# Second attention: keys copied once by ScalarE and spread over the heads by GpSimd; masks handed over by their banks

## What is computed

```python
    def _L2_xattn_ref(query, key, value, Wq, bq, Wk, bk, Wv, bv, Wo, bo):   # 16 heads of 8
        q = (query @ Wq.T + bq).reshape(B, T, H, D).transpose(0, 2, 1, 3)
        k = (key @ Wk.T + bk).reshape(B, S, H, D).transpose(0, 2, 1, 3)
        v = (value @ Wv.T + bv).reshape(B, S, H, D).transpose(0, 2, 1, 3)
        scores = jnp.einsum('bhtd,bhsd->bhts', q, k) / np.sqrt(D)
        scores = scores + causal[None, None]
        attn = jax.nn.softmax(scores, axis=-1)
        out = jnp.einsum('bhts,bhsd->bhtd', attn, v)
        return out.transpose(0, 2, 1, 3).reshape(B, T, E) @ Wo.T + bo
```

## Time and profile before

| | before |
|---|---|
| median of 3 runs | 862.83 us (862.62 to 863.03) |
| profiled execution | 861.2 us, span 859.1 us |
| TensorE busy | 809.4 us (94%) |
| VectorE busy | 625.2 us (73%) |
| ScalarE busy | 581.3 us (68%) |
| GpSimd busy | 271.1 us (32%) |

### The profile page before, as it was taken

One profiled execution on the slowest core, in us unless ns is written; L12 is line 12 of the kernel. 1 busy time (PEld: TensorE's weight loads), 2 busy tenths in 40 slices (PEclk: granted clock), 3 DMA queues, 4 the chain that ended last, 5 costly groups with the idle time before them and its releaser, 6 DMA issues.

```text
span 859.1 us, 20341 instructions
## 1 busy us (share of the span) xinstructions
PE 809.4 (94%) x7364; PEld 563.9 (66%) x7364; DVE 625.2 (73%) x1588; ACT 581.3 (68%) x1645; POOL 271.1 (32%) x571
## 2 busy tenths in 40 slices
PE   9999999999999999899999999999888889899986
PEld 8887888888888986544444444444555564676652
DVE  5677777777777565676785786685877667799876
ACT  3666676776777766776545585545788879778664
POOL 4355445544444444210000000002034230344455
PEclk9999999999999999999999999999999999999999
DMA  8700000000000000000000000000000000000000
GB/s 339 160 2 2 1 2 2 2 2 1 1 2 2 2 1 2 1 1 0 1 1 0 1 2 0 1 1 0 23 7 3 4 2 1 2 4 3 3 19 34
DMA packets 7887, 13.54 MB, mean 16 GB/s; under 512 B 4342, under 2 KB 5100, under 8 KB 7532
## 3 DMA queue, kind: packets, MB, share of 16 engines
q1 hardware_dynamic: 7788, 12.24, 4.5%
HBM read 11.19 MB, written 1.05 MB: 14 GB/s over the span
## 4 chain that ended last, share of the span: by engine, by line
PE 60%; DVE 13%; ACT 12%; POOL 8%; issue 5%; DMA 0%; DVEq 0%; POOLq 0%; SPq 0%; ACTq 0%
PE psum L1564 10%; PE psum L772 6%; PE psum L812 4%; POOL rstd L520 3%; PE psum L755 3%; PE psum L2018 3%; PE psum L764 3%; ACT arena L2096 3%; POOL arena L1100 2%; PE psum L1573 2%; DVE negmax L1010 2%; PE psum L1550 2%; PE psum L840 2%; ACT arena L910 2%; PE psum L2526 2%
## 5 line engine op out<-in xcount | busy, mean ns | idle before, releaser
L517 POOL TENSOR_TENSOR ve<-mv,epsv 128x1 f32<-128x1 f32 x176 | 36.4, 207 | 508.4 <-DVE mv L512 508.4
L1564 PE MATMUL psum<-arena,w1f 128*128 128x512 f32 x240 | 109.5, 592 | 0.0
L520 POOL TENSOR_TENSOR rstd<-ve,epsv 128x1 f32<-128x1 f32 x176 | 101.7, 578 | 13.8
L910 ACT ACTIVATE arena<-psum,negmax 128x128 f32<-128x128 f32 x256 | 90.5, 408 | 22.2 <-DVE negmax L1010 22.2
L1564 PEld LDWEIGHTS psum<-arena,w1f 128*128 128x128 f32 x240 | 45.5, 190 | 48.7 <-issue 44.3
L1100 POOL TENSOR_TENSOR arena<-arena,rsum 128x512 f32<-128x512 f32 x64 | 65.3, 1040 | 5.6 <-DVE rsum L1016 5.6
L910 ACT ACTIVATION_READ_ACCUMULATOR arena<-psum,negmax 128x1 f32 x256 | 63.4, 248 | 0.0
L1010 DVE TENSOR_REDUCE negmax<-psum 128x8 f32<-128x1024 f32 x32 | 39.2, 1225 | 32.9 <-PE psum L812 32.7
L755 PE MATMUL psum<-arena,sclA 128*128 128x128 f32 x512 | 62.5, 275 | 0.1
L772 PE MATMUL psum<-arena 128*128 128x512 f32 x128 | 61.3, 598 | 0.7 <-DVE arena L1005 0.4
L840 PE MATMUL psum<-prjB,arena 128*128 128x128 f32 x512 | 59.9, 275 | 0.0
(11 more groups left out here) (376 smaller groups left out, 1968.4 us busy)
## 6 DMA issues: line engine op xcount, KB each, us to landing
w<-in_w0qk SPq DMA_DIRECT2D x2, 512.0 KB, 5.0
w<-in_w0vo SPq DMA_DIRECT2D x1, 1024.0 KB, 7.6
cT<-in_cT SPq DMA_DIRECT2D x1, 1024.0 KB, 15.8
out<-x_tok SPq DMA_DIRECT2D x4, 256.0 KB, 2.2
rows<-in_rows SPq DMA_DIRECT2D x1, 836.0 KB, 12.3
x_tok<-in_x_tok SPq DMA_DIRECT2D x1, 768.0 KB, 9.8
ctx_tok<-in_ctx_tok SPq DMA_DIRECT2D x1, 768.0 KB, 10.8
wa<-in_wa SPq DMA_DIRECT2D x1, 768.0 KB, 17.4
```

The source lines that it names most:

```text
L520: pool.tensor_tensor(rstd[:, u, self.i:self.i + 1], ve[:, u, self.i:self.i + 1], epsv[:, 1:2], ALU.pow) \
L910: m = nc.scalar.activation(e0[:, b, g, :], ps(k, P, j * P), ACT.Exp, bias=negmax0[:, b, g:g + 1], accum_out=sum0[:, b, g:g + 1])
L1564: nc.tensor.matmul(ps(k), w1("e2", j * 384 + arg * D, j * 384 + (arg + 1) * D), f1_Hm[:, n, 2 * j + i, :], start=False, stop=False)
```

## The change

1. ScalarE's "qk" of the second attention writes the keys once, with the plain bias, to a new pair of tiles `kT2` (128x128 each). `bk2` and its VectorE instruction go.
2. GpSimd gets a new kind "km": one product of 128x512 that spreads `kT2` over four copies and multiplies by `head4`. It waits until ScalarE has released the bank of keys and queries, and until the scores of two tiles before are done. Its semaphore `a2_spread` is a new wait of TensorE before the scores. Its place is lag 2 in `ATT_POOL`, behind "root" and ahead of "tail", and in `POOL_END` three stand before the root of tile 5 and one behind its bias.
3. ScalarE no longer waits for its own mask copies and raises no `f1_kept`; VectorE waits for the bank of the mask in its place.

```diff
-        POOL_END = [..., ("root", 4), ("own", 4), ("root", 5), ("own", 5)]
+        POOL_END = [..., ("root", 4), ("own", 4), ("km", 0), ("km", 1),
+                    ("km", 2), ("root", 5), ("own", 5), ("km", 3)]
-        ATT_POOL = [("root", 0), ("tail", 7), ("bias", 8), ("own", 1)]
+        ATT_POOL = [("root", 0), ("km", 2), ("tail", 7), ("bias", 8), ("own", 1)]
...
                 nc.scalar.activation(f1_mask[n][MASKS.index(arg)], ps(k), ACT.Copy).then_inc(free[k], 1)
-                stored(act, f1, f"m{it}{arg}", t)
-                act.sem_inc(f1_kept, 1)
...
                 if it == 0:
-                    dve.wait_ge(f1_kept, held(c, arg))
+                    stored(dve, f1, f"m{it}{arg}", t)
...
                     stored(pe, a, "qk", t)
                     if n == 3:
                         kept(pe, "K", t)
+                    else:
+                        pe.wait_ge(spread, t.times(1, 1))
...
                     if n == 2:
-                        if t.n == 0:
-                            act.wait_ge(a_half, 4)
-                        for h in range(QUAD):
-                            nc.scalar.activation(km[:, u, :, h, :], ps(k, P, P).rearrange("p (b k) -> p b k", b=2), ACT.Identity,
-                                                 bias=bk2[:, h:h + 1], scale=head4[:, h:h + 1])
+                        nc.scalar.activation(kT2[:, u, :], ps(k, P, P), ACT.Identity, bias=vec("a2_bk"))
                     nc.scalar.activation(qT2[:, u, :], ps(k, P), ACT.Identity, bias=bqs[:, n - 1:n], scale=DH2 ** -0.5).then_inc(free[k], 1)
...
+                if kind == "km":
+                    u = t.n % 2
+                    stored(pool, a, "qk", t)
+                    if t.n == 0:
+                        pool.wait_ge(a_half, 2 * (n - 1))
+                    if t.n >= 2:
+                        filled(pool, a, "s3", t - 2)
+                    pool.tensor_tensor(km[:, u, :, :, :], kT2[:, u, :].rearrange("p (b k) -> p b k", b=2).unsqueeze(2).to_broadcast((P, 2, QUAD, S)),
+                                       head4.unsqueeze(1).unsqueeze(3).to_broadcast((P, 2, QUAD, S)), ALU.mult).then_inc(spread, 1)
```

More of the change, by code:

```diff
@@ L1294, in build @@
                    ("max", 1), ("s", 1), ("own", 5), of_prev("Z"), of_last("G"), ("apply", 5), of_last("Z")]
-        POOL_END = [("root", 0), ("root", 1), ("own", 0), ("own", 1), ("root", 2), ("root", 3), ("own", 2), ("own", 3), ("root", 4), ("own", 4), ("root", 5), ("own", 5)]
+        POOL_END = [("root", 0), ("root", 1), ("own", 0), ("own", 1), ("root", 2), ("root", 3), ("own", 2), ("own", 3), ("root", 4), ("own", 4), ("km", 0), ("km", 1),
+                    ("km", 2), ("root", 5), ("own", 5), ("km", 3)]
         END_BANKS = {("ha1A", PREV): 7, ("ha1B", PREV): 5, ("f21", PREV): 4, ("hh1", LAST): 5, ("f110", LAST): 6, ("f111", LAST): 7,
@@ L1491, in build @@
         F1_CLOCK = {('L', 0, 0, None): 4, ('H', 2, 0, 's'): 7, ('H', 3, 0, 's'): 3, ('F', 3, 1, None): 5, ('Z', 3, 1, None): 4}
-        f1_masked, f1_kept = sem("f1_masked"), sem("f1_kept")
+        f1_masked = sem("f1_masked")
         spare = [arena[:, 16384:16896], mat(rows, ROWS, "f0_s1"), mat(rows, ROWS, "f0_s2"), ctx_tok[:, 1792:2048],
@@ L1501, in masked @@
             return len(MASKS) * [at for at, *_ in turns()].index((c, it)) + MASKS.index(arg) + 1
-        def held(c, arg):
-            return len(MASKS) * c + MASKS.index(arg) + 1
         def f1_pe(pe, x):
@@ L1904, in build @@
         bk3 = sb("bk3", [P, QUAD])
-        bk2 = sb("bk2", [P, QUAD])
         v3_built = sem("v3_built")
@@ L1963, in attention @@
             max2 = carve(2 * H2).rearrange("p (u h) -> p u h", u=2)
+            kT2 = carve(2 * P).rearrange("p (u k) -> p u k", u=2) if late else None
             assert used["n"] <= (24 * C1 if late else ARENA - (2 * 2 * HALF * 18 + HALF + QUAD)), used
             maxed, exped, inverted, spent = (sem(f"a{n}_{x}") for x in ("max", "exp", "rsum", "spent"))
+            spread = sem("a2_spread") if late else None
             def on_pe(pe, kind, n_tile):
@@ L2177, in dve_build @@
                 nc.vector.tensor_scalar(bk3[:, :], head4, vec("a3_bk"), None, ALU.mult).then_inc(a_half, 1)
-                nc.vector.tensor_scalar(bk2[:, :], head4, vec("a2_bk"), None, ALU.mult).then_inc(a_half, 1)
                 nc.vector.tensor_copy(Vx.rearrange("p u g (r c) -> p (u g) r c", c=9)[:, :, :, DH2],
```

## The result

| | before | after |
|---|---|---|
| median of runs, side by side | 862.73 us (862.43 to 863.03, 4 runs) | 849.61 us (849.10 to 850.99, 4 runs) |
| profiled execution | 861.2 us, span 859.1 us | 850.01 us, span 848.0 us |

The ratio is 0.985, with a 95% interval of 0.9833 to 0.9868. In a second comparison it was 0.9854 (0.9827 to 0.9881; 849.31 us in 6 runs). The forecast was 851.0 us, with a range of 848.8 to 855.3. Single executions of one kernel differ by up to some 5 us, in part because the granted clock of TensorE falls for some 3 us in some of them (experiment 6), so small effects are read from places in the traces.

The account below looks back on a forecast made before the run. Waits between engines bound the second attention: 2.80 us on TensorE plus 2.93 on ScalarE per round of 5.73. Gains of 9.9 (steady part), 1.6 (beginning) and 0.3 (masks) make 11.8: 862.8 - 11.8 = 851.0 us, range 848.8 to 855.3.

Parts of the forecast that it names:

- rival without contention: Second attention: the product slides behind "apply", rounds of 4.79 us and 2.1 gained at the beginning: 849.6 us; chance 0.15.
- costliest case inside the range: Product of 1.5 us on GpSimd and a starved first product at the beginning, both: 854.7 us; rival's chance 0.22.
- ScalarE's loop: Second attention: four key copies become one, 1.38 to about 0.26 us, so the loop falls from 5.73 to 4.61 us.
- TensorE's and VectorE's loop: Second attention: transposes, residual sum, masks, scores, values and back to transposes; the next loop to set the round, 4.79 us.
- round with "apply" held: Second attention: VectorE's L526 held until GpSimd's product is done, 0.74 us later, making VectorE's round 4.99 us.
- mean of the nine rounds from t4: Second attention: rounds of 4.79 and 4.99 us alternate, mean 4.89 us, for nine rounds.
- first three rounds together: Second attention's first three rounds, with no outgoing tile yet: estimated at 4.7 us each.
- t1 to t13: Second attention, tile 1's transposes to tile 13's: 12 rounds from 68.02 to 58.1 us, 9.9 gained.
- product on GpSimd: Second attention: the new 128x512 product with both inputs broadcast takes 1.04 us, 1.5 at the range's upper side.
- beginning, to t1: Start of the second attention: 0.55 us gained at L1587 and 1.1 from tile 2's keys, gain 1.6.
- masks: ScalarE's mask copies unguarded: gain 0.3 us at the first chunk, none in three chunks, bounds 0 and 0.7.
- The rival in which GpSimd is the bound: Second attention: mean round 3.30 + (K+1.4)/2, over 5.73 us from product time K = 3.4; about 866 us at K = 4.1; chance 0.04.

Follow-up runs that it names:

- experiment 6: Changed kernel with three small moves (product a tile later, second product late, clock-keeping products 5 to 2): 849.02, again 848.95 us; changed kernel rerun, giving its second trace: 849.31 us.
- experiment 7: No new kernel: TensorE's pause in the last round (5.52 us instead of 4.92), read from the traces of before, the changed kernel and the other runs.
- Experiment 2: Changed kernel with further ScalarE activations of the old keys' form per tile, written where nobody reads: one 850.43 us, three 863.72 us.
- experiment 3: Changed kernel with the keys' product at lag 3 in ATT_POOL instead of 2, for the tile after next: 850.74 us, ratio 0.9852 to before.
- Experiment 4: Changed kernel with each GpSimd keys' product made several times into the same place: twice 853.67 us, three times 873.47 us, four times 892.12 us.
- second product late: Changed kernel where, at the beginning, GpSimd makes the second tile's product only after VectorE's first row maximum: 849.95 us.

## Why the prediction was right

Its total, 11.8 us, stands beside 12.2 us of span in the second trace (859.1 to 846.9); the forecast for the profiled execution, 849.4, beside 849.03 there. The first trace gained 11.1 us of span, and would have gained some 12.7 without its fall of the clock (1.7 us, experiment 6). The medians moved by more, 13.1 us: the sum took over that the median lies 1.6 us above an undisturbed execution, as it does before, and the changed kernel's medians lie 0.6 and 0.3 above it (849.61 and 849.31 against 849.03). Why the changed kernel's runs lie closer to it is open.

The time alone does not confirm the mechanism. The measured 849.61 is the very number of the rival without contention (849.6), which the traces refute: VectorE's L526 is held in each round up to 665 us. The two forecasts differ by 1.4 us, less than single executions do, so it is the rows below that decide. The upper end of the range, 855.3, is not worked out in the prediction; its costliest case inside the range gives 854.7. By its own terms, the measured column from the first trace of the changed kernel:

| term | forecast | measured |
|---|---|---|
| ScalarE's loop | 4.61 | 4.60, from 4.95 less 0.35 and 5.65 less 1.05 of added work |
| TensorE's and VectorE's loop | 4.79 | 4.69 to 4.72 |
| round with "apply" held | 4.99 | 4.92 |
| mean of the nine rounds from t4 | 4.89 | 4.78 |
| first three rounds together | 14.1 | 14.09 (4.46 4.57 5.06) |
| t1 to t13 | 9.9 gained | 10.9 gained |
| product on GpSimd | 1.04 | 1.04; 1.12 and 1.14 beside VectorE's products |
| beginning, to t1 | 1.6 gained | 1.28 gained (1.96 less the 0.68 that was there) |
| masks | 0.3 gained | 0.47 gained |
| last round | 0 | 0.6 lost |

That the first three rounds add up to 14.1 is luck: none of them is the 4.7 of the estimate. The last round was put at no change; what lengthened it is the pause of experiment 7.

**The steady part.** The mechanism held at each step: ScalarE's four copies left the loop, the second loop took over, "apply" was held for the product and the rounds alternated. Experiment 2 shows the first step in numbers: the loop that no longer binds was sized to 0.02 us. The term that was mis-sized is the second loop. Of its stretches L576 and the masks came where the sum had them (t+1.50 and t+2.97 in the round from 661.72), but L2008 at t+4.55 and not at t+4.62, the 0.07 us by which 4.72 falls short of 4.79; the row that was shown as a check, +4.73 at 688.70, was nearer to the truth, and I kept the sum instead of the row. In the held round L576 comes at t+1.70, and all the rest is 0.2 later. Over nine rounds these 0.07 to 0.09 us are 0.7 of the 1.0 us by which the gain was put too small. The rest is that in this trace the alternation ends at 662 us, where VectorE has no incoming tile's statistics left; I had let it run through all nine.

The Trainium skill, "SBUF — State Buffer", section "SBUF: two separate sides", says that GpSimd and VectorE share one pair of ports as an exclusive lock, held for the whole instruction by whichever starts first, and wanted by VectorE only in a two-port mode or with two SBUF inputs. The trace agrees in the main: L526 0.34 to 1.06 us, L1789 and L1790 0.69 to 1.41, none ending before the product, while L2120, which reads PSUM and SBUF, stays at 1.23. It does not show which of the two conditions L526 meets; that one has a single data input in SBUF. And it does not show that the one that starts first goes first: with lag 3, L526 began 0.07 us ahead of the product and was held, while the product took its 1.04 us (experiment 3); in the earlier trace rows, 0.17 us ahead, it was not.

**The beginning.** The three steps to L1584 were right: first scores at 603.74, which is 604.42 in the times of before (604.35 forecast; 0.68 are the shift that was there), VectorE's chain 1.44 us longer (1.35 forecast), 0.49 gained at L1584 (0.55 forecast), and the two products did slip in between VectorE's. What was missing is the pause of 0.43 us in front of L1596; no row of before showed it. With it TensorE's shift is back at -0.67 there, so that all of the 0.49 was given back. The keys of the third tile then gave 1.3 us, a little more than the 1.1 forecast, and that is nearly all of the 1.28: that the total came near 1.6 is in part luck.

**The masks.** 0.47 instead of 0.3, inside the bounds; one step at the first chunk and none in the others, as argued. The spacing of the copies was put at 0.54 us and is 0.48.

**The rival in which GpSimd is the bound** was priced wrongly, though it did not come to pass. Its formula let the product's time into every second round only. Experiment 4 shows it in every round, K + 2.98. The point from which the round is longer than before is K = 2.75 us by that, not 3.4, and K = 1.5, the upper bound that I took for the product, would have cost nothing in this way (4.48, still below 4.70). The chance I gave it, 0.04, rested on the 3% spread of the product in the earlier trace rows, and that was the right row: 14 of the 16 products took 1.04 us.

## What to carry to other kernels

When a stage is bound by a chain through several engines, write down each loop that closes once per tile with its length, and take the next longest as the new round; where the trace holds one round in which the removed work is absent, trust that row more than the sum. Work that is moved to GpSimd costs its time on GpSimd, and here up to 0.7 us more on VectorE where it stood beside L526 or beside a product with two inputs in SBUF; it cost nothing beside L2120 and L576, which read PSUM, or where VectorE had slack in its loop. Before a slow engine is given more work, follow the loop through it to the end and see whether it passes through every round: here one product cost nothing in this loop (4.02 us against 4.70), and two cost 0.45 us in each round (5.15 against 4.70).

## What the hardware showed that I had not expected

- TensorE paused 0.86 and 1.19 us in the middle of a list of 64 small products without any wait (1.04 and 1.37 us from one instruction's start to the next), in each run whose rounds before it took 5.65 us or less, and in no run of 5.73 or more; always behind its 5199th MATMUL, and always until 1.3 to 1.6 us after a packet of instructions had ended. A second pause, 0.43 us in front of L1596, was in the changed kernel and not in before; there the last packet of instructions had ended 22 us earlier.
- A fall of the granted clock (a mean of 0.83 to 0.86 of full in windows of 10 and 12 us, so part of them at 1.2 GHz and the rest at 2.4) costs 1.3 to 1.7 us here, and it comes at different places in executions of kernels that differ little: at 605 us with the masks alone, at 718 us with lag 3, at 815 us in the changed kernel's first trace and in the one with the second product late, at 345 us in the second trace of the three moves, nowhere of weight in the changed kernel's second. That is more than any of the masks, the order of GpSimd and the late second product is worth, so these could be judged from the places in the trace only.
- The product with both inputs spread over four dimensions took 1.04 us in 14 of 16 cases, the same as the one with a single spread input in the earlier trace rows; the other two, 1.12 and 1.14 us, stood beside VectorE's products.
- A VectorE instruction that is held shows a longer time and not a later start, and it does not take its full time behind the product: L526, 0.34 us alone, ended 0.08 us after the product that held it; L1789 and L1790, 0.69 us alone, ended 0.55 us after theirs.
